# A graph message kernel: row fetches by byte address in four pieces, more of them, deferred loads, 14 slots and a shorter drain

## The chip, the core and the metric

The kernel runs on one core of one Trainium2 chip. The metric is device time in microseconds (us), the median of several executions. Engines are named as in the profile: PE (TensorE), DVE (VectorE), ACT (ScalarE), POOL (GpSimd), SP (SyncE). "SPq" and "ACTq" are the instructions with which SP and ACT start DMAs.

## What is computed

One message-passing layer on a graph of 6,250 nodes and 206,250 edges, sorted by receiver, feature width D = 128 in 8 heads of 16:

```python
w_ij = silu(edge_feats @ rad_W1 + rad_b1) @ rad_W2 + rad_b2
w_ij = w_ij + (silu(chi_scalar @ sph_W1 + sph_b1) @ sph_W2 + sph_b2)
q_i = (x @ Wq)[receivers];  k_j = (x @ Wk)[senders];  v_j = (x @ Wv)[senders]
alpha = (q_i * w_ij * k_j).sum(per head) / sqrt(16) * cutoffs
out = segment_sum(alpha * v_j, receivers) / 16
x = layernorm(x + out)
```

## The kernel before

**Prologue.** PE projects all nodes to keys and values; the table `kvtab` in HBM gets one row of 1 KB (key and value, 256 floats) per node. Then it projects the queries, which go to `qtab` as three bf16 parts. In this stretch SP and ACT also bring in index and weight arrays: the sender indices `srcS`, the edge weights `cutS` (which DVE multiplies by 1/64 at L425), the receiver indices, and the tables of row numbers `rowsS` and `rowsA`.

**Main loop.** The edges go in NE = 403 groups of 512 edges, each of four tiles of 128 edges. For a group:
- POOL gathers the sender rows of `kvtab`, one indirect DMA per tile (L540), into one of KS = 13 slots of `kvt`. A slot is free when DVE has made the messages of the group 13 before (wait on `m_msg`). The first HX = 6 groups need no such gather (`kvh`, made in the prologue). For the group in which POOL first uses a slot again, group HX + KS = 19, it waits for the messages of group 6.
- In some groups the fourth tile isn't gathered by POOL. Its 128 rows come one by one, each by a DMA of its own, RS = 7 rows a group from SP into `kvS` (L510) and RA = 8 a group from ACT into `kvA` (L629; 4 behind the two SiLUs of an even group, 12 behind those of an odd one). `row_tiles` says which groups these are: 21 fed by SP and 25 by ACT, so that POOL has 397 x 4 - 46 = 1542 gathers. The row number comes from a register, which a TENSOR_LOAD fills for four groups at once (28 registers on SP, 32 on ACT); a register instruction (named ISA below) makes the address from it.
- SP further issues, for each group, the query rows `qwt` (L516, behind a wait for the queries' matmul `m_q` of five groups earlier), and every four groups the edge features `eft` (L321, ES = 4 buffers) and the receivers `dbt` (L327).
- PE makes the hidden layer (L552, for two groups at once), the second layer `w_ij` (L575, L577), spreads the queries to edges (L565), sums messages by receiver (L585 into one bank, `SB`) and folds the four tiles (L591). ACT applies SiLU (L614). DVE multiplies weights and keys (`t1`, L708), then queries (L716), reduces per head (L718), makes the one-hot matrices (L640, L646), scales by the cutoff (L730), makes messages (L736), copies the sums to `part` (L655) and adds them to `accT` (L662).

PE sums group g - 3 while it works on group g, since `accumulate` of one group must end before the next may write `SB`. After the last group three groups are still to be summed, each by the same round of PE and DVE through the one bank. Then come three updates of window arrays, used only if the program loops again, the barrier, and the layernorm: PE centres (L799), ACT squares and takes roots (L810, L816), DVE scales (L834), SP stores.

What orders the work is the program text of each engine, joined by semaphores.

## Time and profile before

| | us |
|---|---|
| median of 3 runs | 2017.05 |
| lowest, highest | 2016.06, 2017.72 |
| the profiled execution | 2016.91 |
| its span, first to last instruction | 2015.6 |
| mean granted clock of PE | 0.932 of full speed |

| engine | busy us | share of the span |
|---|---|---|
| PE | 1709.1 | 85% |
| DVE | 1495.3 | 74% |
| POOL | 1488.6 | 74% |
| ACT | 560.7 | 28% |

Instructions that issue DMAs, read registers or wait aren't counted as busy, so the busy time of SP, ACT and POOL says little of how full their instruction streams are. The timeline shows the issue instructions of SP and ACT as merged rows: "x7" with 2.80 us is the time from the start of the first to the end of the seventh. For POOL the "idle before" of a gather that waited for nothing is put down to "issue".

### The profile page before, as it was taken

How to read it: one execution, taken by the hardware profiler on the slowest of the kernel's cores; microseconds unless marked ns; L12 is line 12 of the kernel's file. 1: busy time of each engine (PE TensorE's matmuls, PEld its weight loads, DVE VectorE, ACT ScalarE, POOL GpSimd, SP SyncE). 2: the span in 40 equal slices, each digit the busy share in tenths (PEclk: the TensorE clock that was granted, in tenths of full speed). 3: DMA queues.
4: the chain of work that ended last, by engine and by line, in shares of the span. 5: the costliest groups of instructions: out<-in, count | busy, mean ns of one | idle time of the engine just before them, and what ended most of it. 6: DMA issues, size and time to landing. Idle time of an engine off the chain costs nothing. (4 is left out here: it accounts for less than half of the span.)

```text
span 2015.6 us, 59668 instructions
## 1 busy us (share of the span) xinstructions
PE 1709.1 (85%) x14497; PEld 1251.5 (62%) x14497; DVE 1495.3 (74%) x3816; ACT 560.7 (28%) x955; POOL 1488.6 (74%) x1575
## 2 busy tenths in 40 slices
PE   8688989888988888888887888889888888888886
PEld 7566666666666666566665666656656665666665
DVE  4587887888887777777777777768777776777775
ACT  5332322222222222222222222222222222222233
POOL 6767777777777777777777777777777777777772
PEclk9899999999999989989899989988899999899898
DMA  9856666665666656655656656565565656566554
GB/s 330 268 149 164 171 170 170 168 166 160 170 170 171 166 158 168 169 158 163 169 152 169 164 157 169 152 168 162 160 168 152 169 162 159 159 162 169 150 139 127
DMA packets 194752, 339.98 MB, mean 169 GB/s; under 512 B 81140, under 2 KB 107108, under 8 KB 194404
## 3 DMA queue, kind: packets, MB, share of 16 engines
q0 software_dynamic: 74784, 203.79, 37.5%
q1 hardware_dynamic: 112488, 127.77, 21.9%
q10 hardware_dynamic: 7132, 4.59, 1.0%
q8 instruction: 119, 1.95, 0.4%
q14 instruction: 229, 1.88, 0.3%
HBM read 321.03 MB, written 14.95 MB: 167 GB/s over the span
## 5 line engine op out<-in xcount | busy, mean ns | idle before, releaser
L540 POOL DMA_INDIRECT kvt<-kvtab,srcS x1542 | 1462.8, 949 | 482.1 <-issue 458.4
L614 ACT ACTIVATE hs<-bank,B 128x512 f32<-128x512 f32 x806 | 509.9, 684 | 1399.2 <-PE bank L552 954.6
L708 DVE TENSOR_TENSOR t<-bank,kvt 128x512 f32<-128x512 f32 (+1 forms) x397 | 268.3, 676 | 398.3 <-DMA kvt<-kvtab,srcS 218.1
L575 PE MATMUL bank<-W2r,hs 128*128 128x128 f32 x3224 | 512.8, 307 | 8.9 <-ACT hs L614 8.9
L575 PEld LDWEIGHTS bank<-W2r,hs 128*128 128x128 f32 x3224 | 430.7, 208 | 97.2 <-issue 79.2
L575 PE MATMUL bank<-W2s,hs 128*128 128x128 f32 x3224 | 460.5, 290 | 0.0
L575 PEld LDWEIGHTS bank<-W2s,hs 128*128 128x128 f32 x3224 | 429.6, 207 | 0.0
L585 PE MATMUL bank<-msg,oh 128*32 128x128 f32 x3224 | 180.9, 296 | 245.3 <-DVE accT L662 240.7
L585 PEld LDWEIGHTS bank<-msg,oh 128*32 128x32 f32 x3224 | 71.9, 110 | 437.5 <-issue 437.5
L718 DVE TENSOR_REDUCE bank<-t 128x32 f32<-128x512 f32 x403 | 279.9, 695 | 13.9
L716 DVE TENSOR_TENSOR t<-bank,t 128x512 f32<-128x512 f32 x403 | 273.3, 678 | 17.5 <-PE bank L565 16.4
L736 DVE TENSOR_TENSOR msg<-kvt,bank 128x512 f32<-128x512 f32 (+1 forms) x397 | 266.6, 671 | 13.6
L552 PE MATMUL bank<-eft,W 32*128 32x512 f32 x1612 | 243.0, 671 | 0.9 <-DMA eft<-in_ef 0.9
L591 PEld LDWEIGHTS bank<-cS,part 128*128 128x128 f32 x806 | 122.5, 191 | 97.2 <-issue 94.0
L565 PE MATMUL bank<-qwt,ot 96*128 96x128 bf16 x1612 | 159.4, 221 | 23.8 <-issue 23.7
L591 PE MATMUL bank<-cS,part 128*128 128x32 f32 x806 | 167.6, 291 | 2.0 <-DVE part L655 2.0
L577 PE MATMUL bank<-b2p,ones 3*128 3x512 bf16 x403 | 158.5, 393 | 0.0
L640 DVE TENSOR_SCALAR ot<-dbt,basep 96x512 bf16<-96x512 int16 x403 | 150.2, 373 | 8.8 <-DMA qtab<-qx 8.1
L565 PEld LDWEIGHTS bank<-qwt,ot 96*128 96x128 bf16 x1612 | 131.1, 119 | 26.0 <-issue 26.0
L655 DVE COPY part<-bank 128x128 f32<-128x128 f32 x403 | 114.0, 283 | 13.1 <-PE bank L585 13.0
L646 DVE TENSOR_TENSOR oh<-cS,rel 128x128 f32<-128x128 f32 x403 | 114.0, 283 | 0.0
L552 PEld LDWEIGHTS bank<-eft,W 32*128 32x128 f32 x1612 | 65.8, 190 | 23.6 <-issue 2.2
(79 smaller groups left out, 491.4 us busy)
## 6 DMA issues: line engine op xcount, KB each, us to landing
eft<-in_ef SPq DMA_DIRECT2D x103, 512.0 KB
kvA<-kvtab ACTq DMA_DIRECT2D x3200, 1.0 KB
kvS<-kvtab SPq DMA_DIRECT2D x2688, 1.0 KB
dbt<-dst SPq DMA_DIRECT2D x102, 384.0 KB
kvt<-kvtab,srcS POOLq DMA_INDIRECT x1542
qwt<-qtab SPq DMA_DIRECT2D x403, 24.0 KB
kvtab<-kvt SPq DMA_DIRECT2D x24, 256.0 KB, 7.1
qtab<-qx SPq DMA_DIRECT2D x12, 384.0 KB, 8.6
```

The lines of the kernel that those rows point to most:

```text
L540: pool.indirect_dma_start(kvt[:, (g - HX) % KS, t, :], None, kvtab, bass.IndirectOffsetOnAxis(ap=srcS[:, g * TG + t:g * TG + t + 1], axis= ...
L552: pe.matmul(HB[i][:, :], W1[32 * i:32 * i + 32, :], eft[32 * i:32 * i + 32, q % ES, p % 2, :], start=True, stop=True).then_inc(m_l1, 1)
L565: m = pe.matmul(QB[:, t * D:(t + 1) * D], ot[:, g % OS, t * 128:(t + 1) * 128], qwt[:, g % QS, :], start=True, stop=True)
L575: pe.matmul(WB[g % 2][:, t * D:(t + 1) * D], hs[:, g % HS, j, t * 128:(t + 1) * 128], w2[:, :], start=(j == 0 and t == 0), stop=False, ski ...
L577: pe.matmul(WB[g % 2][:, :], ones3[:, :], b2p[:, :], start=False, stop=True, skip_group_check=True).then_inc(m_w, 1)
L585: m = pe.matmul(SB[32 * t:32 * t + W, 0:D], oh[:, g % MS, t, :], msg[:, g % MS, t, :], start=True, stop=True)
L591: pe.matmul(SB[:, D:D + W], part[:, g % 2, :], fold, start=True, stop=True).then_inc(m_fold, 1)
L614: act.activation(hs[:, g % HS, j, :], HB[i % 4][:, :], ACT.Silu, bias=B1[:, j:j + 1]).then_inc(m_si, 1)
L708: m = dve.tensor_tensor(t1[:, s, a:b, :], tiles(WB[s][:, :])[:, a:b, :], kv[:, :, 0:D], ALU.mult)
L716: dve.tensor_tensor(t2[:, s, :, :], tiles(QB[:, :]), t1[:, s, :, :], ALU.mult).then_inc(m_t2, 1)
L718: dve.tensor_reduce(alpha(g), t2[:, s, :, :].rearrange("p t (h d) -> p (t h) d", h=H), AX.X, ALU.add).then_inc(m_rd, 1)
L736: m = dve.tensor_tensor(msg[:, g % MS, a:b, :].rearrange("p t (h d) -> p t h d", h=H), kv[:, :, D:2 * D].rearrange("p t (h d) -> p t h d", ...
```

## The change

- RS and RA go from 7 and 8 to 9 and 10. 28 groups get their fourth tile from SP and 31 from ACT, POOL has 397 x 4 - 59 = 1529 gathers. Fetched tiles now lie in groups 15, 16, 28, 30, ...; the last two groups, 401 and 402, have four gathers each (402 had three).
- DVE multiplies the row numbers by 1024 in the prologue, so that a register holds the byte offset, and the DMA takes it directly. The register instruction in front of each row fetch goes, and of each `qwt` DMA too (`baseq`). A row is described as 4 x 256 bytes on both sides; `kvS` and `kvA` are laid out so. The registers are filled for two groups at once, 20 of them (18 used on SP, 20 on ACT).
- KS goes from 13 to 14, ES from 4 to 3.
- The bulk of `srcS` and `cutS` is loaded by ACT after its part of the query projection, where SP loaded both in the middle of it; the first 64 columns of `cutS` still come from SP. The factor 1/64 moves into the constant `fold`, and DVE's multiplication and its wait for `cutS` go.
- The last two groups are summed in banks of their own (`strips`), so that their sums don't wait for `accumulate`; the window updates are placed between steps that wait; `oh` of the last group and the update of `rel` come ahead of its wait for the gather.
- The two instructions of DVE for a fetched tile take it as two halves of 64 floats.
- After the barrier ACT takes one root of a constant (`rooted`) ahead of the layernorm's squares, so that the function table is loaded there.

```diff
-RS, RA = 7, 8
+RS, RA = 9, 10
+LS, LA = -(-2 * RS // 4) * 4, -(-2 * RA // 4) * 4
...
-    KS, ES, DS, QS, HS, MS, OS = 13, 4, 3, 6, 4, 4, 3
+    KS, ES, DS, QS, HS, MS, OS = 14, 3, 3, 6, 4, 4, 3
...
+    KVROW, QROW = 4 * 2 * D, 2 * NPART * D
+    kv_bytes = kvtab.rearrange("n f -> (n f)").bitcast(u8)
+    q_bytes = qtab.rearrange("n f -> (n f)").bitcast(u8)
...
-        rowsS = sb("rowsS", [NG // 4, 4 * RS], i32)
-        rowsA = sb("rowsA", [NG // 4, 4 * RA], i32)
-        kvS = sb("kvS", [128, 2, 2 * D], f32)
-        kvA = sb("kvA", [128, 2, 2 * D], f32)
+        rowsS = sb("rowsS", [NG // 4, 2 * LS], i32)
+        rowsA = sb("rowsA", [NG // 4, 2 * LA], i32)
+        kvS = sb("kvS", [128, 4, 2, D // 2], f32)
+        kvA = sb("kvA", [128, 4, 2, D // 2], f32)
         kvt = sb("kvt", [128, KS, TG, 2 * D], f32)
-        dbt = sb("dbt", [WP, DS, 4, G], i16)
+        dbt = sb("dbt", [128, DS, 4, G], i16)
...
-                if b == min(9, NQB):
-                    dve.wait_ge(s_cut, 16)
-                    dve.tensor_scalar(cutS[:, :], cutS[:, :], 1.0 / 64.0, None, ALU.mult).then_inc(s_win, 1)
...
-                if b == min(4, NQB - 1):
-                    sp.dma_start(srcS[:, SE:T], srcT[:, SE:T]).then_inc(s_src2, 16)
                 if b == min(5, NQB - 1):
-                    sp.dma_start(cutS[:, :], cutT).then_inc(s_cut, 16)
+                    sp.dma_start(cutS[:, 0:SE], cutT[:, 0:SE]).then_inc(s_cut, 16)
...
-                    features(1)
+            if NQP > 1:
+                features(1)
             dve.wait_ge(s_win, 4)
 
+            act.dma_start(srcS[:, SE:T], srcT[:, SE:T]).then_inc(s_src2, 16)
+            act.dma_start(cutS[:, SE:T], cutT[:, SE:T]).then_inc(s_cut2, 16)
+            dve.wait_ge(s_rows, 32)
+            for rows in (rowsS, rowsA):
+                dve.tensor_scalar(rows[:, :], rows[:, :], float(KVROW), None, ALU.mult).then_inc(s_bytes, 1)
+            dve.wait_ge(s_cut, 16)
...
+            def kv_row(reg):
+                return kv_bytes[bass.ds(start_of(reg, (N - 1) * KVROW), KVROW)].rearrange("(o a f) -> o a f", o=1, a=4)
 
             def sp_rows(g):
-                if g % 4 == 0:
-                    sp.load(sp_row, rowsS[g // 4:g // 4 + 1, :])
+                if g % 2 == 0:
+                    sp.load(sp_row, rowsS[g // 4:g // 4 + 1, g % 4 // 2 * LS:(g % 4 // 2 + 1) * LS])
                 for r in range(RS * g, RS * (g + 1)):
                     u, p = r // 128, r % 128
                     if u < len(at_s):
                         if p == 0 and u >= 2:
                             sp.wait_ge(m_msg, at_s[u - 2] + 1)
-                        row = sp.snap(sp_row[r % (4 * RS)], min_val=0, max_val=N - 1)
-                        sp.dma_start(kvS[p:p + 1, u % 2, :], kvtab[bass.ds(row, 1), :]).then_inc(m_kvS[u % 2], 16)
+                        sp.dma_start(kvS[p:p + 1, :, u % 2, :].bitcast(u8), kv_row(sp_row[r % (2 * RS)])
+                                     ).then_inc(m_kvS[u % 2], 16)
 
             def query_rows(g):
                 if g >= QS:
                     sp.wait_ge(m_q, g - QS + 1)
-                at = window_start(sp, sp_base, g)
-                sp.dma_start(qwt[:, g % QS, :],
-                             qtab[bass.ds(at, W), :].rearrange("n (c f) -> (n c) f", c=NPART)
+                if g % 4 == 0:
+                    sp.load(sp_base, baseq[0:1, g:g + 4])
+                at = start_of(sp_base[g % 4], (NQ - W) * QROW)
+                sp.dma_start(qwt[:, g % QS, :].bitcast(u8),
+                             q_bytes[bass.ds(at, W * QROW)].rearrange("(n f) -> n f", n=W * NPART)
...
+            def strips(g):
+                return HB[NE - 1 - g] if g >= NE - 2 else SB
+
             def scat(g):
                 pe.wait_ge(m_msg, g + 1)
-                if g >= 1:
+                if g >= NE - 2:
+                    pe.wait_ge(m_si, 2 * NE)
+                elif g >= 1:
                     pe.wait_ge(m_acc, g)
                 for t in range(TG):
-                    m = pe.matmul(SB[32 * t:32 * t + W, 0:D], oh[:, g % MS, t, :], msg[:, g % MS, t, :],
+                    m = pe.matmul(strips(g)[32 * t:32 * t + W, 0:D], oh[:, g % MS, t, :], msg[:, g % MS, t, :],
                                   start=True, stop=True)
                 m.then_inc(m_sc, 1)
 
             def fold_tiles(g):
                 pe.wait_ge(m_part, g + 1)
-                pe.matmul(SB[:, D:D + W], part[:, g % 2, :], fold, start=True, stop=True).then_inc(m_fold, 1)
+                pe.matmul(strips(g)[:, D:D + W], part[:, g % 2, :], fold, start=True, stop=True).then_inc(m_fold, 1)
...
+            scat(NE - 3)
+            scat(NE - 2)
+            fold_tiles(NE - 3)
+            fold_tiles(NE - 2)
+            scat(NE - 1)
+            fold_tiles(NE - 1)
...
+            def next_rel():
+                dve.wait_ge(m_oh, NE)
+                dve.tensor_scalar(rel[:, :], rel[:, :], -float(W), None, ALU.add).then_inc(m_up, 1)
...
+            def next_base():
                 dve.wait_ge(m_q, NE)
-                dve.wait_ge(m_oh, NE)
                 dve.tensor_scalar(base[:, :], base[:, :], float(W), None, ALU.add).then_inc(m_up, 1)
+                dve.wait_ge(m_up, 2)
+                dve.tensor_copy(basei[:, :], base[0:1, :]).then_inc(m_up, 1)
+                dve.tensor_scalar(baseq[:, :], base[0:1, :], float(QROW), None, ALU.mult).then_inc(m_up, 1)
+
+            def next_basep():
                 dve.tensor_scalar(basep[:, :], basep[:, :], float(W), None, ALU.add).then_inc(m_up, 1)
-                dve.tensor_scalar(rel[:, :], rel[:, :], -float(W), None, ALU.add).then_inc(m_up, 1)
...
+                if g == NE - 1:
                     window(g)
-                if g == NE:
-                    next_windows()
-                if g >= NE:
+                    next_rel()
...
+                n, kv, row = gathered(g), kv_rows(g), alone(g)
+                m = dve.tensor_tensor(t1[:, s, 0:n, :], tiles(WB[s][:, :])[:, 0:n, :], kv[:, 0:n, 0:D], ALU.mult)
+                if row is not None:
+                    m = dve.tensor_tensor(halves(t1[:, s, KT, :]), halves(WB[s][:, KT * D:TG * D]), row[:, 0:2, :],
+                                          ALU.mult)
...
+            collect(NE - 2)
+            accumulate(NE - 3)
+            accumulate(NE - 2)
+            next_base()
+            collect(NE - 1)
+            next_basep()
+            accumulate(NE - 1)
...
+            act.activation(rooted[:, :], eps[:, :], ACT.Sqrt)
...
-    cst[:, 4 + W + 256:] = np.tile(np.eye(W), (128 // W, 1))
+    cst[:, 4 + W + 256:] = np.tile(np.eye(W), (128 // W, 1)) / 64.0
```

The two streams of SP in the steady loop, one row per instruction: `kvS` is a row fetch, ISA the register instruction, `qwt` the query rows. Before:

```order
L510 DMA kvS<-kvtab 1x256
L499 ISA
L516 DMA qwt<-qtab 96x128
L509 ISA
L510 DMA kvS<-kvtab 1x256
```

SP in the changed kernel, for four groups (L328 is `eft`, L334 `dbt`):

```order
L528 DMA qwt<-qtab 96x256
L328 DMA eft<-in_ef 128x2x512
L334 DMA dbt<-dst 96x2048
L513 TENSOR_LOAD rowsS
L519 DMA kvS<-kvtab 1x4x256 x9
L528 DMA qwt<-qtab 96x256
L519 DMA kvS<-kvtab 1x4x256 x9
L528 DMA qwt<-qtab 96x256
L513 TENSOR_LOAD rowsS
L519 DMA kvS<-kvtab 1x4x256 x9
```

The register instructions are gone, nine fetches follow each other directly, and there are two loads of registers for four groups where there was one.

PE at the end of the loop, where L585 sums a group's messages and L591 folds them; before:

```order
L565 MATMUL bank<-qwt,ot 128x128 x4
L585 MATMUL bank<-msg,oh 32x128 x4
L591 MATMUL bank<-cS,part 128x32
L585 MATMUL bank<-msg,oh 32x128 x4
L591 MATMUL bank<-cS,part 128x32
L585 MATMUL bank<-msg,oh 32x128 x4
L591 MATMUL bank<-cS,part 128x32
```

And in the changed kernel (L602 and L608):

```order
L577 MATMUL bank<-qwt,ot 128x128 x4
L602 MATMUL bank<-msg,oh 32x128 x8
L608 MATMUL bank<-cS,part 128x32 x2
L602 MATMUL bank<-msg,oh 32x128 x4
L608 MATMUL bank<-cS,part 128x32
```

Groups 400 and 401 are now summed one behind the other, and only group 402 makes a round of its own.

## Rows read from the trace of the kernel before

**Rows 1.** The page's costliest groups: POOL's gathers.

```profile
L540 POOL DMA_INDIRECT kvt<-kvtab,srcS x1542 | 1462.8, 949 | 482.1 <-issue 458.4
```

**Rows 2.** Waits of the whole span: total us, times, longest us.

```profile
POOL kvt L540 <- issue: 458.4, 1503, 0.3
DVE t L708 <- DMA kvt<-kvtab,srcS: 218.1, 129, 4.4
DVE t L708 <- PE bank L577: 180.2, 222, 4.8
POOL kvt L540 <- DVE msg L736: 19.1, 38, 6.3
```

**Rows 3.** Timeline of POOL: start us, us, operation, idle before and releaser.

```profile
39.47 0.94 POOL L540 DMA_INDIRECT kvt<-kvtab,srcS  x1 [4.62 <-DMA kvtab<-kvt]
...
110.46 0.94 POOL L540 DMA_INDIRECT kvt<-kvtab,srcS  x1 [6.30 <-DVE msg L736]
...
116.84 0.95 POOL L540 DMA_INDIRECT kvt<-kvtab,srcS  x1 [1.68 <-DVE msg L736]
...
1978.81 0.95 POOL L540 DMA_INDIRECT kvt<-kvtab,srcS  x1 [0.30 <-issue]
```

**Rows 4.** Timeline of SP's issues in the loop, four groups' special ones among them.

```profile
87.61 2.74 SPq L510 DMA_DIRECT2D kvS<-kvtab  x7
91.16 0.32 SPq L516 DMA_DIRECT2D qwt<-qtab  x1
...
1504.13 0.44 SPq L321 DMA_DIRECT2D eft<-in_ef  x1
1504.62 0.49 SPq L327 DMA_DIRECT2D dbt<-dst  x1
1507.22 2.80 SPq L510 DMA_DIRECT2D kvS<-kvtab  x7
```

**Rows 5.** Timeline of ACT's issues: a load onto three partitions, row fetches.

```profile
3.25 0.25 ACTq L214 DMA_DIRECT2D b2w<-in_b2s  x1
...
1510.96 0.63 ACTq L629 DMA_DIRECT2D kvA<-kvtab  x2
...
1511.76 3.81 ACTq L629 DMA_DIRECT2D kvA<-kvtab  x10
```

**Rows 6.** Timeline of the prologue's end.

```profile
61.73 1.00 DVE L425 TENSOR_SCALAR cutS<-cutS 128x1616 f32<-128x1616 f32 x1 [5.89 <-DMA cutS<-in_cutT]
...
76.47 0.61 DVE L640 TENSOR_SCALAR ot<-dbt,basep 96x512 bf16<-96x512 int16 x2 [8.15 <-DMA qtab<-qx]
```

**Rows 7.** Timeline of the last group and the drain.

```profile
1981.64 0.56 DVE L708 TENSOR_TENSOR t<-bank,kvt 128x384 f32<-128x384 f32 x1 [0.40 <-DMA kvt<-kvtab,srcS]
...
1984.85 0.28 DVE L736 TENSOR_TENSOR msg<-kvA,bank 128x128 f32<-128x128 f32 x1
...
1987.55 0.29 DVE L655 COPY part<-bank 128x128 f32<-128x128 f32 x1 [0.86 <-PE bank L585]
...
1988.67 0.19 DVE L662 TENSOR_TENSOR accT<-accT,bank 128x32 f32 x1 [0.83 <-PE bank L591]
...
1990.94 0.35 DVE L743 CAST basei<-base 1x404 int32<-1x404 f32 x1
...
1992.64 12.89 PE L799 MATMUL bank<-cS,accT 128*128 128x128 f32 x98 [1.94 <-PEq L751]
```

**Rows 8.** The chain that ended last, in order of time: the layernorm's start.

```profile
1992.64 3.75 PE bank L799 x16
...
1997.58 1.28 ACT L816
...
1998.87 0.31 ACT sd L816
```

**Rows 9.** Stretch of the main loop: us, busy per engine, clock, DMA share, GB/s.

```profile
81.00:1979.00 1898.00, 1631.34 (x14031) 1183.37 (x14030) 1439.66 (x3697) 508.09 (x804) 1430.30 (x1510) 0.94 0.60 162
```

More of the change, by code:

```diff
@@ L104, in gnn_program @@
         basei = sb("basei", [1, NG], i32)
+        baseq = sb("baseq", [1, NG], i32)
         npass = sb("npass", [1, 1], i32)
@@ L679, in kv_rows, with alone, halves @@
                 return kvt[:, (g - HX) % KS, :, :]
[L681 to L682 removed]
+            def alone(g):
                 if g in use_s:
[L684 removed]
+                    return kvS[:, :, use_s[g] % 2, :]
                 if g in use_a:
[L686 to L687 removed]
+                    return kvA[:, :, use_a[g] % 2, :]
+                return None
+            def halves(t):
+                return t.rearrange("p (c f) -> p c f", c=2)
             def alpha(g):
```

161 lines of the change are left out of this document (79 added, 82 removed).

## The prediction, made before the changed kernel ran

> **What bounds the kernel now.** The share of busy time points at PE (85%) and says little, so I read the waits first. DVE's first step of a group waits 218.1 us for gathered rows, in 129 of 397 groups, and 180.2 us for PE [rows 2]. A wait for rows can come from late transfers or from late issue, so the second view is POOL. It has 1542 gathers of 949 ns, and 458.4 us of idle time between them in pieces of at most 0.3 us, which is its own issue time [rows 1, 2]. The timeline gives the sum directly: from the first gather at 39.47 to the last at 1978.81 are 1939.3 us for 1541 steps [rows 3]. POOL really waited in only two places worth naming, 6.30 and 1.68 us, of which 0.30 each is the ordinary gap: 7.4 us, both before 117 us, when its slots had filled ahead of the first groups. So a step costs (1939.3 - 7.4) / 1541 = 1.2537 us, and after 117 us POOL never pauses for anyone. When PE falls behind, as in the stretches of low clock, DVE lags some groups and catches up; that costs nothing as long as POOL isn't stopped by full slots, and it isn't.
>
> The time is therefore: start of the gathers (39.5), 1542 steps, the first stalls, and what follows the last gather. The last gather starts at 1978.81, its group begins on DVE at 1981.64, the last update is done at 1991.3, PE's centring starts at 1992.64 [rows 3, 7], and the layernorm ends the span at 2015.6.
>
> **The change, part by part**, against the profiled execution's own 2016.91 us (1.3 above its span, 0.14 below the median of 2017.05, so nothing has to be shifted).
>
> 1. *Fewer gathers.* 1542 - 1529 = 13 steps of 1.2537 us: **-16.3**. They lie on the path that sets the end, all of them. The instruction itself is the same.
>
> 2. *The first stalls.* POOL was ready for slot 1's second use at 110.46 - 6.00 = 104.5 and got it at 110.46. With a fourteenth slot, and two fetched tiles (groups 15, 16) before that point where one was (18), it makes 54 gathers first and not 51, and asks at 108.2. It then wants the messages of group 7 at 113.2, which came at 116.5. So without any faster start 3.3 us of stall remain of 7.4. The start should be faster too: DVE's wait of 5.89 us for `cutS` and the 1.0 us multiplication go [rows 6]. The next step needed the queries' projection, which other waits held as well, so I count that the query chain is some 3 us or more ahead and the two big loads no longer delay the last writes of `qtab`, for which DVE waited 8.15 us until 76.47 [rows 6]. 3.3 us earlier is enough to end the stall. Against it: ACT now issues the loads just behind, beside those same writes. Bounds: all 7.4 gained, or, if the start comes 4 us later, nothing. I take **-7.4**, since the cleared wait is in a row and the delay isn't.
>
> 3. *The drain.* From the last gather to its group's first step nothing changes (2.83 us, landing). `oh` and the update of `rel` are put ahead of it; group 401 had its rows four gathers, 5.0 us, earlier, and needs 3.4 us (1981.64 to 1985.13, rows 7), so the 1.1 us fit in the gap and cover is there. With full four tiles and without `oh`, group 402 is some 0.3 shorter. After its messages (1985.13): before, 6.2 us to the end of the last cast. Now: copy to fold to update for group 401, as in 1987.55 to 1988.67, 1.1 us plus 0.2; then base, basei and baseq at 0.35 each, 1.1; meanwhile PE has summed group 402; then copy, fold, update again, 1.3. That makes 3.8 and not 6.2 [rows 7]. **-2.7** together; bounds 0 (if the two new waits cost as much as they save) and -3.5.
>
> 4. *The root.* The table load of 1.28 us stands in the chain between squares and first root [rows 8]; ahead of the squares it lies under PE's first centring, 3.75 us for two blocks in the chain. After it DVE is the busy one to the end, so everything moves up: **-1.3**. The Trainium skill ("ScalarE: Activation LUTs", What ACT_TABLE_LOAD costs) gives 2.66 us for a switch, the load and a drain of 1.38. The row shows the load alone, with 0.01 us behind it. By the page the sum would be 1.4 us lower.
>
> 5. *What SP and ACT pay for the rates.* This decides whether part 1 stands. Two fetches take 0.63 us and ten 3.81 [rows 5]: one each (3.81 - 0.63) / 8 = 0.40, the issue itself 0.23, the rest gap and register instruction. Without that instruction only a gap as between two plain issues stays, 0.05 (eft to dbt, rows 4). How long the issue of four pieces is no row shows. Below: 0.23 (one piece). Above: 0.32, the 96 pieces of `qwt` [rows 4]. Nearest: 0.25, a load onto three partitions [rows 5]. So a fetch costs p = 0.28 to 0.37, and I take 0.30, less than the 0.40 now. Registers: the load of 28 took 1507.22 - 1505.11 = 2.11, less an ordinary 0.19, 1.92; the one of 4 took 0.62 (91.16 - 90.35, less 0.19); 20 are then about 1.5. For four groups SP has 36 fetches, four `qwt` with their gaps (0.42 each), `eft` and `dbt` (1.03), two loads of 20 and one of 4: 36p + 1.7 + 1.03 + 3.0 + 0.6 = 36p + 6.3, so 17.1 us at 0.30. From its start at about 77 to the end of the gathers at 1955 a group may take (1955 - 77) / 403 = 4.66, four of them 18.6. It fits, with 1.5 us left; before it was about 17.6 of 18.9. ACT has 20p + 1.5 = 7.5 for two groups beside its SiLUs, before 16 x 0.40 + 1.1 = 7.5. Cost **0**, covered by POOL; the cover is gone at p = 0.34.
>
> 6. *The rest at nothing.* ES = 3 makes SP wait at every fourth group until PE's first layer of the group before is done: it is then three to four groups ahead and not five, and behind that wait stand `dbt`, a register load and nine fetches, wanted four groups later. DVE's two halves have the same element count, and DVE waits for rows anyway. POOL needs the rest of `srcS` at its group 16, at about 88; ACT issues that load before 70. More pieces for the queues: their engines are busy 0.60 of the loop [rows 9].
>
> Sum: 16.3 + 7.4 + 2.7 + 1.3 = 27.7, and 2016.9 - 27.7 = **1989.2 us**, 1.4% faster.
>
> **Rivals.**
>
> - *A. SP becomes the bound (slower).* Place: the row fetches and `qwt` behind them, for which PE's L565 would wait in every group. Price: each 0.01 us of p above 0.34 adds 0.09 us a group, 36 us in all. Slower than before from p = 0.35. At the upper bound 0.37 a group takes 4.9 us and the time is about 1989 + 403 x 0.25 = 2090. For it: the margin is 8% and the issue of this form is in no row. Against it: the three-piece load at 0.25, and that a piece count of 96 only gives 0.32. Chance 0.10.
>
> - *B. The first stall stays*, since the deferred 1.6 MB come down on the last `qtab` writes: 1989.2 + 7.4 = 1996.6, or 1992.5 if only the slot helps. For it: DVE waited 8.15 us for their landing while bulk loads ran. Chance 0.20.
>
> - *C. The gathers stretch.* Every row now is four pieces, 30,208 where there were 5,888; they use the same transfer engines as POOL's gathers. If a step grows by 0.01 us, 1529 of them cost 15: about 2004. Against it: at a DMA share of 0.60 [rows 9] the mean step, 1.2537, is 949 ns and the 0.30 of issue to within 0.005 [rows 1, 3]: nothing stretched it so far. The Trainium skill ("DMA: Bandwidth & Descriptors", Specifications) says that below 512 bytes a transfer is read, modified and written, which speaks against such pieces; no row here times one piece alone. Chance 0.06.
>
> - *D. The change doesn't do what it says*, or PE's pace hides the 13 gathers: between 2013 and 2017. But the count of gathers is fixed by the plan, and PE is busy 1631 us and DVE 1440 us in the loop's 403 groups, 4.05 and 3.57 us a group [rows 9], under the 4.66. Chance 0.02.
>
> **How the numbers follow.** The forecast (1984 to 1994) has 0.62. Its lower end adds the larger bounds of parts 3 and 4, about 1985, and 1984 for a step nearer 1.250. With B the mass reaches 1998; half of C lies within 1999. Range 1984 to 1999 leaves out A, D and the rest of C, and a little at the low end. A measurement of this kernel tells 0.2% from no change: faster by more than that has 0.62 + 0.20 + 0.06 = 0.88, the same 0.02, slower 0.10.
>
> **What would show it.** Right: POOL's gathers x1529 at 949 ns, first start near 39.5, last near 1955; its waits for DVE near nothing; DVE still waits for rows, not for `qwt` or `kvS`; fetches of 0.30 us, nine in under 2.8; 11 us and not 13.8 from the last gather to PE's centring; no table load behind the squares. Wrong: PE waiting for DMA at the queries' matmul, DVE's L742 released by `kvS` or `kvA`, or POOL's step above 1.26.

## The result, and the profile after

| | us |
|---|---|
| kernel before, median of 4 runs of the comparison | 2017.38 (2016.06 to 2020.03) |
| changed kernel, median of 4 runs | 3542.88 (3540.14 to 3548.99) |
| ratio, with its 95% interval | 1.756 (1.7535 to 1.759) |
| profiled execution, its span | 3544.71, 3543.0 |

The change makes the kernel slower by 1525 us. The forecast was 1989.2 and the range ended at 1999. The likeliest case was wrong. The rival "SP becomes the bound" had the right kind of cause, the issue of the row fetches, but a price far too low and, for the changed kernel itself, the wrong place: PE waits for ACT there and not at the queries' matmul.

The costliest groups of the changed kernel (same columns as [rows 1]; the releaser at the end is what ended most of the idle time). L552 is what L540 was, L635 the SiLUs, L587 the second layer, L742 DVE's first step of a group:

```profile
L552 POOL DMA_INDIRECT kvt<-kvtab,srcS x1529 | 1447.1, 946 | 1945.2 <-DVE msg L770 1318.0
...
L635 ACT ACTIVATE hs<-bank,B 128x512 f32<-128x512 f32 x806 | 509.3, 683 | 2937.2 <-issue 2076.2
L742 DVE TENSOR_TENSOR t<-bank,kvt 128x512 f32<-128x512 f32 (+1 forms) x397 | 266.6, 671 | 1594.3 <-PE bank L589 1267.6
```

And its waits (total us, times, longest), to be read against [rows 2]:

```profile
ACT hs L635 <- issue: 2076.2, 225, 10.5
POOL kvt L552 <- DVE msg L770: 1318.0, 299, 29.0
DVE t L742 <- PE bank L589: 1275.1, 298, 8.4
...
PE bank L587 <- ACT hs L635: 763.1, 194, 11.8
...
ACT hs L635 <- PE bank L589: 801.1, 169, 5.3
```

Read backwards this is one queue. POOL's 1529 gathers still take 946 ns each, but now POOL stands 1318 us waiting for DVE to free slots. DVE waits 1275 us for PE's second layer, PE waits 763 us for the hidden layer from ACT, and ACT waits 2076 us for "issue", that is for nothing but its own instruction stream. The 801 us that are put down to PE's L589 are of the same kind: the idle time of an engine counts its own DMA issues in. In the timeline below the SiLU at 1506.59 has 4.66 us of it, and ACT's fifth fetch before it ended at 1506.48. Taken instruction by instruction, with issues and register loads counted as occupied, ACT's stream waits for another engine nowhere between 110 and 3498 us (no gap over 0.35 us). The timeline of ACT and SP shows what fills that stream (start us, us, operation; idle before and releaser):

```profile
1500.67 1.26 ACT L635 ACTIVATE hs<-bank,B 128x512 f32<-128x512 f32 x2 [10.02 <-issue]
...
1501.98 2.08 PE L587 MATMUL bank<-W2r,hs 128*128 128x128 f32 x8 [4.49 <-ACT hs L635]
...
1502.71 3.77 ACTq L649 DMA_DIRECT2D kvA<-kvtab  x5
1503.21 6.83 SPq L519 DMA_DIRECT2D kvS<-kvtab  x9
...
1506.59 0.69 ACT L635 ACTIVATE hs<-bank,B 128x512 f32<-128x512 f32 x1 [4.66 <-PE bank L589]
1506.69 0.58 ACTq L649 DMA_DIRECT2D kvA<-kvtab  x1
...
1507.37 10.25 ACTq L649 DMA_DIRECT2D kvA<-kvtab  x14
...
1511.68 6.37 SPq L519 DMA_DIRECT2D kvS<-kvtab  x9
1517.72 1.26 ACT L635 ACTIVATE hs<-bank,B 128x512 f32<-128x512 f32 x2 [9.87 <-issue]
```

One fetch costs 0.58 us by itself and 0.71 to 0.76 in a row of them, where ten took 3.81 before, register instructions included [rows 5], and where the prediction took 0.30. From 1500.67 to 1517.72, two groups of ACT, are 17.05 us, of which 3.77 + 0.58 + 10.25 = 14.6 us are twenty fetches; a register load of 1.9 us takes most of the rest. At this pace the loop's 201.5 pairs of groups take 3436 of the 3543 us. SP is full as well: its `eft` of every fourth group stands at these times, 29 cycles apart:

```profile
315.14 0.43 SPq L328 DMA_DIRECT2D eft<-in_ef  x1
...
1312.65 0.42 SPq L328 DMA_DIRECT2D eft<-in_ef  x1
```

(1312.65 - 315.14) / 29 = 34.40 us for four groups, 8.60 each. Before, SP's cycle had room. Its waits in the kernel before, for the queries' matmul:

```profile
SPq L498 <- PE bank L565: 79.5, 35, 5.5
SPq L499 <- PE bank L565: 79.0, 47, 7.3
```

In the changed kernel nothing of the kind is left: the longest wait of SP in the loop is 0.5 us. So both streams are full, and over the loop they run at one pace, 17.2 us for two groups on ACT and 34.4 for four on SP. PE waits for ACT alone; its queries' matmul L577, for which SP fetches, has 0.2 us of wait. Why two streams of different content run at the same pace isn't shown.

The stretch of the loop, to be read against [rows 9] (us, busy of PE, weight loads, DVE, ACT, POOL, granted clock, DMA share, GB/s):

```profile
81.00:3500.00 3419.00, 2542.64 (x13932) 1833.90 (x13932) 1454.85 (x3697) 504.81 (x800) 1415.38 (x1497) 0.66 0.32 90
```

DVE and POOL do the same work as before (1455 and 1415 us). The transfer engines are busy 0.32 of the time and not 0.60, so the loss isn't in moving bytes. PE's busy time grew from 1631 to 2543 us because the granted clock fell from 0.94 to 0.66 of full speed, in a loop in which PE stood waiting for ACT: the eight matmuls of L587 in the timeline above take 2.08 us, at the lower of its two levels (1.2 GHz) and behind a wait of 4.49, where they take 1.16 in the one-piece kernels below at the higher (2.4 GHz). The lower clock doesn't set the time: ACT's stream never waits for PE there, and PE still has 763 us of wait for ACT left over.

### The profile page after: what moved, and what is told of

The parts are those of the page before. It is cut to its first block and busy times, and to the rows that moved or that the text cites. A ratio compares the mean times of both kernels' runs of the same rounds, so it can differ in the third digit from the quotient of the medians.

```text
span 3543.0 us, 56930 instructions
## 1 busy us (share of the span) xinstructions
PE 2629.3 (74%) x14497; PEld 1908.5 (54%) x14497; DVE 1520.9 (43%) x3845; ACT 560.3 (16%) x956; POOL 1472.3 (42%) x1562
## 5 line engine op out<-in xcount | busy, mean ns | idle before, releaser
L552 POOL DMA_INDIRECT kvt<-kvtab,srcS x1529 | 1447.1, 946 | 1945.2 <-DVE msg L770 1318.0
L587 PE MATMUL bank<-W2r,hs 128*128 128x128 f32 x3224 | 788.9, 421 | 786.7 <-ACT hs L635 763.1
L587 PEld LDWEIGHTS bank<-W2r,hs 128*128 128x128 f32 x3224 | 675.4, 310 | 913.5 <-ACT hs L635 823.4
L635 ACT ACTIVATE hs<-bank,B 128x512 f32<-128x512 f32 x806 | 509.3, 683 | 2937.2 <-issue 2076.2
L742 DVE TENSOR_TENSOR t<-bank,kvt 128x512 f32<-128x512 f32 (+1 forms) x397 | 266.6, 671 | 1594.3 <-PE bank L589 1267.6
L587 PE MATMUL bank<-W2s,hs 128*128 128x128 f32 x3224 | 693.6, 388 | 4.7 <-issue 4.7
L587 PEld LDWEIGHTS bank<-W2s,hs 128*128 128x128 f32 x3224 | 670.7, 306 | 4.5 <-issue 4.4
L564 PE MATMUL bank<-eft,W 32*128 32x512 f32 x1612 | 548.7, 890 | 5.1 <-ACT hs L635 2.4
L602 PE MATMUL bank<-msg,oh 128*32 128x128 f32 x3224 | 210.5, 340 | 95.6 <-DVE accT L685 48.2
L564 PEld LDWEIGHTS bank<-eft,W 32*128 32x128 f32 x1612 | 207.4, 243 | 122.6 <-ACT hs L635 79.5
L602 PEld LDWEIGHTS bank<-msg,oh 128*32 128x32 f32 x3224 | 76.6, 121 | 365.3 <-issue 364.5
L608 PEld LDWEIGHTS bank<-cS,part 128*128 128x128 f32 x806 | 146.5, 228 | 130.6 <-issue 126.6
L608 PE MATMUL bank<-cS,part 128*128 128x32 f32 x806 | 194.2, 327 | 2.4 <-DVE part L676 2.4
L589 PE MATMUL bank<-b2p,ones 3*128 3x512 bf16 x403 | 193.0, 479 | 0.3 <-issue 0.3
L577 PE MATMUL bank<-qwt,ot 96*128 96x128 bf16 x1612 | 183.7, 246 | 0.2 <-DVE t L753 0.2
L577 PEld LDWEIGHTS bank<-qwt,ot 96*128 96x128 bf16 x1612 | 158.4, 137 | 1.1 <-DVE t L753 0.7
```

Source lines behind the costliest of these rows:

```text
L552: pool.indirect_dma_start(kvt[:, (g - HX) % KS, t, :], None, kvtab, bass.IndirectOffsetOnAxis(ap=srcS[:, g * TG + t:g * TG + t + 1], axis= ...
L564: pe.matmul(HB[i][:, :], W1[32 * i:32 * i + 32, :], eft[32 * i:32 * i + 32, q % ES, p % 2, :], start=True, stop=True).then_inc(m_l1, 1)
L577: m = pe.matmul(QB[:, t * D:(t + 1) * D], ot[:, g % OS, t * 128:(t + 1) * 128], qwt[:, g % QS, :], start=True, stop=True)
L587: pe.matmul(WB[g % 2][:, t * D:(t + 1) * D], hs[:, g % HS, j, t * 128:(t + 1) * 128], w2[:, :], start=(j == 0 and t == 0), stop=False, ski ...
L589: pe.matmul(WB[g % 2][:, :], ones3[:, :], b2p[:, :], start=False, stop=True, skip_group_check=True).then_inc(m_w, 1)
L602: m = pe.matmul(strips(g)[32 * t:32 * t + W, 0:D], oh[:, g % MS, t, :], msg[:, g % MS, t, :], start=True, stop=True)
```

## The experiments

**The two kernels again.** A repeat of both, each against the kernel before.

> The kernel before itself, unchanged, for its trace on this chip. On two chips every kernel with rows in one piece stood near 3080 us, this one too, and in their traces the transfers issued by SP and ACT stood still for 5 to 12 us at a time, some 90 times in all, while POOL's gathers went on. If that belongs to the chip and not to an edit, this trace shows the same standstills where the time is near 3080, and none where it is near 2017.

Measured: 2015.55 us, beside 2017.79 for the kernel before in that comparison.

> The changed kernel itself, unchanged. Theory: it is bound by SP's and ACT's own issue of the four-piece fetches, 0.66 to 0.78 us each, so its time hardly depends on the chip: 3540 us within 3%, where the kernel before has 2017 and where it has 3080. Rival: it pays the standstills of a slow chip on top, 3540 + 1000.

Measured: 3544.07 us. ACT again waits 2112.0 us for its own issues and POOL 1318.9 us for DVE. The result is a property of the kernel.

**One piece and not four.** This undoes the piece count alone; byte addresses, 9 and 10 rows, slots, loads and drain stay:

```diff
-        kvS = sb("kvS", [128, 4, 2, D // 2], f32)
-        kvA = sb("kvA", [128, 4, 2, D // 2], f32)
+        kvS = sb("kvS", [128, 2, 2 * D], f32)
+        kvA = sb("kvA", [128, 2, 2 * D], f32)
...
-                return kv_bytes[bass.ds(start_of(reg, (N - 1) * KVROW), KVROW)].rearrange("(o a f) -> o a f", o=1, a=4)
+                return kv_bytes[bass.ds(start_of(reg, (N - 1) * KVROW), KVROW)].rearrange("(o f) -> o f", o=1)
```

> The change with each row fetch as one piece of 1024 bytes on both sides, all else as in the change (byte addresses, 9 and 10 rows a group, 14 slots, loads, drain). On another chip such a fetch took 0.31 to 0.33 us in a row of them, inside my bounds. Theory (the pieces alone turned the sign): SP's four groups are 36 x 0.32 + 6.3 = 17.8 us, under the 18.6 that POOL's pace allows, and the parts of the prediction other than the piece count hold: 1989 us, between 1984 and 1999; after the last gather 36 us or so instead of 37.7. Rival (9 and 10 rows a group are too many for SP and ACT whatever their form): over 2030 us, ACT hs and DVE waiting for issue. Rival (the saving of gathers is eaten by other waits): within 0.2% of the kernel before.

Measured: 2061.34 us (2060.0 to 2062.51), the kernel before 2016.94; ratio 1.0222 (1.0204 to 1.0239). Of 1525 us of loss the pieces alone carry 1481. But it isn't the 1989 of my theory either: it is the first rival of this run. What waits is another engine than that rival said: the queries' matmul, behind SP's stream (rows below). So the prediction had two faults, and the second would have turned its sign alone.

**The same at 7 and 8 rows.**

```diff
-RS, RA = 9, 10
+RS, RA = 7, 8
```

> As e11_one_piece, but with 7 and 8 rows a group as in the kernel before, so that POOL has 1542 gathers again. By the prediction's terms this leaves the first stalls (7.4), the drain (2.7) and the root (1.3): 2016.9 - 11.4 = 2005.5 us, and 16.3 us more than e11_one_piece. If it is as fast as e11_one_piece, the thirteen gathers bring nothing; if it is level with the kernel before, the other edits bring nothing.

Measured: 2007.05 us (2006.22 to 2008.66), ratio 0.9951 (0.9935 to 0.9968). The expected 2005.5 is 1.6 away: the edits other than fetches, taken together, bring about what was forecast. Its trace lets me read each of them (below).

**Four pieces in the kernel before**, all else as before; DVE takes the fetched tile in halves.

```diff
-        kvS = sb("kvS", [128, 2, 2 * D], f32)
-        kvA = sb("kvA", [128, 2, 2 * D], f32)
+        kvS = sb("kvS", [128, 4, 2, D // 2], f32)
+        kvA = sb("kvA", [128, 4, 2, D // 2], f32)
...
-                        sp.dma_start(kvS[p:p + 1, u % 2, :], kvtab[bass.ds(row, 1), :])
+                        sp.dma_start(kvS[p:p + 1, :, u % 2, :], kvtab[bass.ds(row, 1), :].rearrange("o (a f) -> o a f", a=4))
```

> The kernel before with one edit: each row fetch described as 4 x 256 bytes, kvS and kvA laid out for it, DVE taking the fetched tile in halves. Rates, addresses, slots, loads and drain as before. Theory (a description of more than one dimension costs SP and ACT a fixed time at each issue): a fetch and its register instruction took 0.76 us in a row of them on another chip; SP's four groups are 28 x (0.66 to 0.80) + 6.3 = 24.8 to 28.7 us, 6.2 to 7.2 a group, so 2580 to 2980 us. Rival (the pieces cost only together with the higher rates or the byte addresses): within 2% of the kernel before.

Measured: 3002.14 us in one run, 22 us above the upper end of what was expected (2580 to 2980). The pieces need neither the byte addresses nor the higher rates to do their harm, and with elements of 4 bytes a lone fetch costs the same 0.58 us. Timeline of SP and ACT:

```profile
1503.07 5.33 SPq L510 DMA_DIRECT2D kvS<-kvtab  x7
1503.11 8.06 ACTq L629 DMA_DIRECT2D kvA<-kvtab  x11
...
1520.35 0.58 ACTq L629 DMA_DIRECT2D kvA<-kvtab  x1
```

Seven fetches take 5.33 us where the same line took 2.80 [rows 4]. With seven and eight rows SP's stream is the longer one, and here PE waits where the rival had said, at the queries' matmul L565:

```profile
PE bank L565 <- issue: 770.7, 239, 7.2
```

That it is SP's issue stream that it waits for shows in the timeline: at nine in ten of these waits it starts 1.7 to 2.8 us behind the issue of its `qwt` rows, which take 1.9 us to land. In the changed kernel it starts 13 us behind (medians).

**Two pieces of 512 bytes** in the changed kernel.

```diff
-        kvS = sb("kvS", [128, 4, 2, D // 2], f32)
+        kvS = sb("kvS", [128, 2, 2, D], f32)
...
-                return kv_bytes[bass.ds(start_of(reg, (N - 1) * KVROW), KVROW)].rearrange("(o a f) -> o a f", o=1, a=4)
+                return kv_bytes[bass.ds(start_of(reg, (N - 1) * KVROW), KVROW)].rearrange("(o a f) -> o a f", o=1, a=2)
```

> The change with two pieces of 512 bytes instead of four of 256. Theory (the cost is that of the second dimension, whatever its count): as slow as the change, 3543 us within some 2%. Rival (each piece has its price, as by the count of packets): half of the loss, about 2760 us. Second rival (pieces under 512 bytes are what is slow): near e11_one_piece.

Measured: 3518.49 us in one run. Half the pieces, the same time: the price isn't one for each piece. Timeline rows of SP and ACT:

```profile
1508.76 6.62 SPq L519 DMA_DIRECT2D kvS<-kvtab  x9
1511.46 0.57 ACTq L649 DMA_DIRECT2D kvA<-kvtab  x1
1512.12 10.10 ACTq L649 DMA_DIRECT2D kvA<-kvtab  x14
```

0.57 us alone and 10.10 for fourteen, against 0.58 and 10.25 with four pieces. The page's queue of ACT says that the pieces themselves were made as written (packets, MB, share): before, changed, two pieces.

```profile
q10 hardware_dynamic: 7132, 4.59, 1.0%
```

```profile
q10 hardware_dynamic: 32764, 7.02, 1.0%
```

```profile
q10 hardware_dynamic: 16892, 6.99, 0.7%
```

With one piece and the changed kernel's rates (the one-piece kernel above) that row has 8956 packets. 3968 fetches with two pieces add 7936, two each, and with four pieces 23808, six each: every piece brings a packet of data and one of completion. The Trainium skill ("DMA: Bandwidth & Descriptors", Why a DMA increments its semaphore by 16 and not by 1) says that such a copy runs on the largest number of engines up to 16 that divides the outermost count on both sides, and that each of them posts its own completion; the packet counts agree. The number of packets doubles between these two kernels and the issue costs the same, so it isn't their number that SP and ACT pay for. No run has pieces on one side of the copy alone, so which side costs is open.

**Which engine binds at 9 and 10 rows.** Four kernels as the one-piece kernel with other rates, one line each: `RS, RA = 9, 8`, `7, 10`, `8, 9` and `8, 10`. In their comparison the kernel before took 2020.62 us (2015.31 to 2023.29), so the ratios say more than the times.

> The change with rows in one piece, 9 rows a group on SP and 8 on ACT, 1535 gathers. Theory (SP's stream of issues is the bound at 9 rows: four groups take 36 x 0.335 + 6.5 = 18.6 us plus about 0.9 of stretched issues, measured 4.87 us a group from the first group on): still about 2040 to 2061 us. Rival (ACT's ten rows are what is too many): 2007.05 - 7 x 1.2537 = 1998.3 us.

Measured: 2004.71 us in two runs, ratio 0.9919 (0.9899 to 0.9939). My theory falls: nine rows on SP beside eight on ACT do no harm.

> As e15, with 7 rows a group on SP and 10 on ACT, 1536 gathers. Theory: SP's four groups are 28 x 0.335 + 6.5 = 15.9 us, POOL stays the bound: 2007.05 - 6 x 1.2537 = 1999.5 us. Rival (ACT is the bound at 10): about 2045 to 2061 us.

Measured: 2004.65 us (1997.86 to 2007.65), ratio 0.9924 (0.9907 to 0.994). Ten rows on ACT beside seven on SP do none either.

> As e15, with 8 and 9 rows a group, 1535 gathers. Theory: SP's four groups are 32 x 0.335 + 6.5 = 17.2 us, 18.1 with the stretch of e11, of 18.7 that POOL's pace allows: 2007.05 - 7 x 1.2537 = 1998.3 us, with next to no margin. Rival (the stretched issues grow with the two rates and pass the allowance): over 2010 us.

Measured: 2003.39 us (1998.83 to 2005.07), ratio 0.9915 (0.9899 to 0.9932).

> As e15, with 8 and 10 rows a group, 1532 gathers. Theory (SP alone decides): 2007.05 - 10 x 1.2537 = 1994.5 us. Rival (ACT's ten rows beside SP's eight stretch SP's issues): over 2005 us.

Measured: 2003.28 us (2000.76 to 2005.4), ratio 0.9908 (0.9891 to 0.9924), between the theory's 1994.5 and the rival's 2005.

So it takes both. The traces say how. `eft` times of SP, first the kernel with 9 and 10 rows, 51 cycles apart:

```profile
300.72 0.42 SPq L328 DMA_DIRECT2D eft<-in_ef  x1
...
1294.75 0.42 SPq L328 DMA_DIRECT2D eft<-in_ef  x1
```

then 9 and 8 rows, 54 cycles apart:

```profile
294.84 0.42 SPq L328 DMA_DIRECT2D eft<-in_ef  x1
...
1287.77 0.42 SPq L328 DMA_DIRECT2D eft<-in_ef  x1
```

Four groups cost SP 994.03 / 51 = 19.49 us with ten rows on ACT and 992.93 / 54 = 18.39 with eight. The prediction allowed 18.6. SP's instructions are the same in both, but its nine fetches take longer. With ten rows on ACT the 398 runs of nine fetches have a median of 2.91 us and a mean of 3.16 (longest ones over 6); with eight they have 2.85 and 2.91. Four of them at 0.25 more make the 1.0 us. One long run of nine, timeline of the kernel with 9 and 10 rows:

```profile
1512.67 2.85 SPq L519 DMA_DIRECT2D kvS<-kvtab  x9
...
1517.50 6.39 SPq L519 DMA_DIRECT2D kvS<-kvtab  x9
```

In the long run of nine single issues of SP lasted 1.42 and 1.34 us where the ordinary one is 0.23; there is no wait in it. ACT's issues beside it stayed at 0.235 us until 1520.3. What the runs of fetches of SP lie above their median in all goes with ACT's rate: 15 us at 7 and 8 rows and 21 at 9 and 8, 31 at 8 and 9, 60 at 7 and 10, 84 at 8 and 10, 102 at 9 and 10. At 7 or 8 rows SP has room for them. Overlap with ACT's fetches alone doesn't bring them: at 7 and 8 rows 374 of SP's 384 runs of fetches overlap ACT's and none is stretched by over 0.6 us.

The trace has one thing more that goes with them. A `qwt` load is spread over the transfer engines and tells its end by sixteen completions, one by one. From its issue to the fifteenth and to the sixteenth (medians of the loads behind 200 us of which all sixteen are in the trace; the last column is the time above the median from the paragraph before):

| kernel, rows of SP and ACT | fifteenth us | sixteenth us | stretched us |
|---|---|---|---|
| kernel before, 7 and 8 | 1.97 | 4.50 | 12 |
| one piece, 7 and 8 | 1.94 | 4.90 | 15 |
| one piece, 9 and 8 | 1.89 | 5.01 | 21 |
| one piece, 8 and 9 | 1.92 | 7.27 | 31 |
| one piece, 7 and 10 | 2.01 | 7.28 | 60 |
| one piece, 8 and 10 | 1.91 | 13.97 | 84 |
| one piece, 9 and 10 | 1.97 | 15.25 | 102 |
| four pieces, 9 and 10 | 2.00 | 2.08 | |

So one of the sixteen parts of a load comes late, and only with fetches in one piece. The likely reading is that these fetches all run on one transfer engine, which has too much to do while the other fifteen have room. The data packets of ACT's fetches with 9 and 10 rows fit it: they come one at a time (1 of 3923 overlaps another), where with four pieces 4203 of 15753 overlap. The trace doesn't name the engine of a packet, so that reading is argued. SP's stretched issues stand where the late part is latest: with 9 and 10 rows 66 of the 85 issues of over 0.6 us come when `qwt` lands over 12 us late, with 8 and 10 rows 64 of 70. That the full engine holds up the issue fits this, but no run shows it by itself.

What waits for SP is the queries' matmul L577, by its `qwt` rows. At each of the 90 waits of over 0.5 us with 9 and 10 rows it starts 0.09 us behind their landing, though SP had issued them 15 to 19 us before. SP itself waits for nothing, and its stream with the stretched issues has the pace of the kernel (4 x 4.87 us); whether SP or a full engine sets that pace can't be told apart here. The waits of the kernel with 9 and 10 rows:

```profile
PE bank L577 <- issue: 203.6, 94, 5.6
...
DVE t L753 <- PE bank L577: 161.6, 88, 4.8
```

and of the one with 9 and 8:

```profile
PE bank L577 <- issue: 59.6, 37, 3.1
DVE t L753 <- PE bank L577: 44.9, 27, 3.0
```

**The same kernels on two other chips.** Eight runs, made ahead of the others, fell on two chips on which the kernel before itself takes 3080 to 3096 us, so that the sign of a small change there can't be carried over. Their expectations were made before this was known, and no time below is to be held against them. The names say which of the kernels above it is: one piece, four pieces only, two pieces, one piece at 7 and 8 rows.

> The changed kernel, but each fetched row is described as one piece of 1024 bytes (kvS and kvA laid out as before); byte addresses from the register, rates 9 and 10, deferred loads, 14 slots and the short drain stay. Theory 1 (issuing four pieces is what costs; after, a fetch takes about 0.76 us of SP's and ACT's stream): a fetch costs 0.28 to 0.30, POOL bounds again, 1989 us. Rival 2 (taking the byte address straight from the register, or fetches with no register instruction between them, is what costs): it stays near 3540 us. Rival 3 (one-byte elements cost, whatever the pieces): also near 3540.

Measured: 3098.68 us, the kernel before 3096.14 there; ratio 1.0015 (0.9997 to 1.0034).

> The kernel before, rates 7 and 8, register instruction kept, 4-byte elements, and only the pieces changed: each row lands as four pieces of 256 bytes in kvS and kvA. Theory 1: a fetch then costs 0.76 us or, with the register instruction on top, up to 0.9. SP has 28 fetches and 6.3 us of other work for four groups, so 27.6 to 31.5 us, 6.9 to 7.9 a group, 403 groups and 120 us around them: 2900 to 3300 us. Rivals 2 and 3 (direct address, one-byte elements): 2017 us, as before.

Measured: 3632.82 us in one run.

> The changed kernel with two pieces of 512 bytes a row in place of four of 256. If the issue's cost goes by the number of pieces (0.23 for one, about 0.7 for four with both queues at work), two take 0.39 and with the gap 0.45: SP 36 x 0.45 + 6.3 = 22.5 us for four groups, 5.6 a group, 2380 us. If it is a fixed price for a second dimension, whatever its size, about 3540. If pieces below 512 bytes were the cost (read, modify, write), 1989.

Measured: 3919.66 us in one run.

> The changed kernel with one piece a row and the old rates 7 and 8, so the deferred loads, the 14 slots, the drain, the root and the byte addresses alone. By the parts of the prediction: 2016.9 - 7.4 (first stalls) - 2.7 (drain) - 1.3 (root) = 2005.5 us. If the deferred loads hold up the start, 2013.

Measured: 3084.70 us, ratio 0.9955 (0.9937 to 0.9973).

On the second chip the kernel before took 3079.95 us.

> The changed kernel with one piece of 1024 bytes a row, once more, beside a run of the kernel before at 2017 (in the first comparison every kernel, the one before too, ran above 3000 us on its chip). A single fetch with one piece took 0.23 us there and with two or four pieces 0.57 and 0.58. Theory 1, now: a second dimension in the description costs 0.34 us an issue, whatever its size, and this alone makes the change slow. Then this kernel takes 1989 us, as the prediction's other parts say. Rival 2 (direct addresses or the higher rates cost as well): between 2017 and 3540.

Measured: 3072.46 us, ratio 0.9975 (0.9955 to 0.9995).

> The kernel before, only with four pieces a row. Theory 1: a fetch costs 0.66 (0.58 and a gap) to 0.80 us. SP 28 fetches and 6.3 us for four groups, 6.2 to 7.2 us a group: 2620 to 3020 us. Rival 2: 2017.

Measured: 3622.32 us in one run.

> The changed kernel with one piece a row and rates 7 and 8: deferred loads, 14 slots, drain, root and byte addresses without the 13 gathers. By the prediction's parts 2005.5 us; 16.3 above the kernel with one piece and rates 9 and 10.

Measured: 3055.11 us, ratio 0.9923 (0.9899 to 0.9947).

The eighth run takes the changed kernel and gives ACT's rows one piece, so that SP alone has four:

```diff
-                        act.dma_start(kvA[p:p + 1, :, u % 2, :].bitcast(u8), kv_row(act_row[r % (2 * RA)])
+                        act.dma_start(kvA[p:p + 1, u % 2, :].bitcast(u8), kv_whole(act_row[r % (2 * RA)])
```

> The changed kernel with four pieces on SP's rows alone; ACT's rows come in one piece. In the changed kernel a lone fetch took 0.58 us, but nine on SP 6.8, 0.78 each, while ACT issued too. If the rest is the two queues hindering each other in the longer form, SP's nine now take 0.66 each, 5.9 us, 36 x 0.66 + 6.3 = 30 for four groups, 7.5 a group, 3140 us. If it is SP's own, 0.78 and 3540.

Measured: 3419.17 us in one run. That lies between the expected 3140 and 3540. Nine of SP's fetches took a median of 6.06 us there, 0.67 each, where the changed kernel has 6.50 with both queues in pieces. So SP's own pieces make the most of its price, and ACT's add some. SP's pieces alone also bind the kernel, at 8.12 us a group beside 8.60 in the changed one: PE again waits at the queries' matmul, L580 in this kernel.

```profile
PE bank L580 <- issue: 945.9, 233, 8.1
```

The counterpart, four pieces on ACT alone, has no run.

What those two chips did shows in the one-piece kernel at 7 and 8 rows on the first of them. Its waits, and a stretch of its timeline:

```profile
DVE t L742 <- remote: 879.8, 126, 8.7
PE bank L602 <- DVE accT L685: 807.5, 164, 9.2
ACT hs L635 <- remote: 760.0, 77, 14.3
```

```profile
1498.87 0.95 POOL L552 DMA_INDIRECT kvt<-kvtab,srcS  x1 [0.30 <-issue]
...
1503.87 0.94 POOL L552 DMA_INDIRECT kvt<-kvtab,srcS  x1 [0.30 <-issue]
1506.64 0.00 SPq L528 DMA_DIRECT2D qwt<-qtab  x1
1506.84 0.69 DVE L742 TENSOR_TENSOR t<-bank,kvt 128x512 f32<-128x512 f32 x1 [8.48 <-remote]
1506.97 1.26 ACT L635 ACTIVATE hs<-bank,B 128x512 f32<-128x512 f32 x2 [10.65 <-remote]
```

Transfers that SP and ACT had issued all but stood still for 5 to 12 us at a time while POOL's gathers went on at their 1.25 us. SP's queue has 33 to 82 gaps of over 5 us between its packets in each of the four one-piece runs on these chips, and none to four in the one-piece runs on the others. With two or four pieces the queue has at most four such gaps, on any chip. The gaps don't add up to the 1050 us by which these chips are slower (the longer ones make at most 690 us in a run). Why stays open.

## Where the prediction was right and where it failed

**Part 5 failed, in its bound.** The structure held: four groups of SP cost 36p + 6.3 us and the cover ends at 18.6. With 9 and 8 rows SP's cycle of 18.39 is 36 x 0.332 + 6.4 (nine fetches in 2.91 us and their gap, by nine). What failed is "So a fetch costs p = 0.28 to 0.37". Its upper end came from `qwt` with 96 pieces and its likely value from a load onto three partitions [rows 4, 5]; both lie one piece to a partition. No row of the trace of before has several pieces within a single partition. It has rows with several in each of 128 partitions, and the prediction passed them over (issues of `eft` with two pieces a partition and of `out` with four; least, median and longest ns):

```profile
L321 SPq DMA_DIRECT2D eft<-in_ef x103: 379/427/1551, 58.0 to 1993.2; - x103
...
L849 SPq DMA_DIRECT2D out<-kvt x12: 372/372/1038, 2000.1 to 2011.6; - x12
```

And the other load onto three partitions, just ahead of the one that gave 0.25, took more than twice as long:

```profile
L214 ACTq DMA_DIRECT2D b2w<-in_b2r x1: 568/568/568, 2.7 to 2.7; - x1
```

At 0.43 and the gap of 0.05 the rival's formula already gives 2487 us. Even these rows don't show 0.58, so the bound had to stay open above, and the rival needed more than 0.10. The measured 34.40 us is p = 0.78 by the prediction's sum (the fetches and their gaps take 0.74 each, and the other work 7.8 us and not 6.3). Put into the rival's own formula, 1989 + 403 x (34.40 / 4 - 4.66) = 3577 us, 1% from the result. So the price was mis-sized by more than a factor of two.

The rival's place came true only where SP's stream is the longer one (pieces at 7 and 8 rows, or on SP alone). In the changed kernel the step "ACT has 20p + 1.5 = 7.5 for two groups" failed with it: fetches and register load take 16.5 us there, and it is ACT for which PE waits.

**The cover was thinner than it looked.** "It fits, with 1.5 us left" used 17.1 us. Its gap of 0.05 us between two fetches came from `eft` and `dbt` [rows 4]. Both kernels have one more register instruction, a MOVE, in front of each fetch, and the change takes out only the other. The kernel with one piece and 9 and 10 rows (least, median and longest ns):

```profile
L519 SPq MOVE kvS<-kvtab x3584: 29/29/29, 77.0 to 2004.0; - x200
```

So the gap is 0.10, and a fetch of one piece costs 0.33 and not 0.28 to 0.30: at the 0.34 where the cover ends. With one piece SP needs 18.4, and 19.5 when ACT issues ten rows a group. By the same formula 19.49 gives 1989 + 403 x 0.21 = 2075; measured 2061. A stream filled to 92% by a sum of unloaded issue times had no room for issues that stretch under load, which no row of the loop before showed either: SP's seven fetches there have a median of 2.78 us and lie 12 us above it in all. Nor did part 5 or part 6 ask whether one of the sixteen transfer engines could be full while they are busy 0.60 on average; the late sixteenth completion says that one nearly was, before the change too. The "about 17.6 us" that SP needed before the change come to 16.5 from the terms named (28 x 0.40 + 1.7 + 1.03 + 1.92 + 0.6); nothing else rests on them.

**Part 1, the gathers, holds.** The step stays at 1.250 to 1.258 us in every kernel where POOL doesn't wait. From 7 and 8 rows to 8 and 9, seven gathers fewer, the last gather moves from 1972.88 to 1964.58, 8.3 us for an expected 8.8. In the kernel with 9 and 10 rows it stands at 1977.33, because POOL then waits for slots, and from there to the end are 81 us and not 33: the gathers had stopped being the bound.

**Parts 2 to 4 can be read in the one-piece kernel with 7 and 8 rows.** Timeline rows of its POOL, DVE, PE and ACT:

```profile
39.78 0.94 POOL L552 DMA_INDIRECT kvt<-kvtab,srcS  x1 [4.83 <-issue]
...
78.36 0.69 DVE L742 TENSOR_TENSOR t<-bank,kvh 128x512 f32<-128x512 f32 x1 [4.38 <-PE bank L589]
...
1972.88 0.95 POOL L552 DMA_INDIRECT kvt<-kvtab,srcS  x1 [0.30 <-issue]
...
1984.26 1.28 ACT L863 ACT_TABLE_LOAD   x1 [15.69 <-PEq L794]
1984.43 2.92 PE L842 MATMUL bank<-cS,accT 128*128 128x128 f32 x12 [1.32 <-PEq L794]
```

| part | predicted us | measured us | how |
|---|---|---|---|
| 2, first stalls | -7.4 | -5.9 | last gather 1978.81 to 1972.88; no wait for slots is left |
| 3, drain | -2.7 | -2.3 | last gather to PE's centring, 13.83 [rows 3, 7] to 11.55 |
| 4, root | -1.3 | -1.1 | centring to the end of the span, 22.96 to 21.87 |

Part 2 came 1.5 short: the first gather starts 0.3 us later, and two of the first four gathers last 0.5 to 0.6 us longer. The time of the last gather and the two stretches behind it make up the whole span, so their -9.3 is the whole difference, 2015.6 to 2006.3. For part 4 the 2.66 us of the Trainium skill ("ScalarE: Activation LUTs", What ACT_TABLE_LOAD costs) would have been too much; the load alone, as [rows 8] show it, is what went. Rival B, that the first stall stays, didn't come: the loop's first L742 runs at 78.36 us, where it ran at 81.89 before.

**Part 6 at nothing is right, as far as it can be read.** In this kernel SP does wait at L328, 318.0 us in 86 places, since `eft` has three buffers, and nothing waits for it: PE's L577 has no wait row of note. Transfers cost nothing extra either (rival C): gathers of 946 ns beside the four pieces. The rule of the Trainium skill ("DMA: Bandwidth & Descriptors", Specifications) on transfers below 512 bytes can't be the cause: two pieces of 512 cost as much as four of 256.

**What remains of the change.** Everything but the four pieces and the highest rates is worth having. One piece with 8 and 10 rows is at 0.9908 of the kernel before (0.9891 to 0.9924), with 8 and 9 at 0.9915 (0.9899 to 0.9932), and both beat the two kernels that were compared. They can't be told apart, nor from 9 and 8 or 7 and 10. The sums had 1994.5 and 1998.3 us for them, ratios 0.989 and 0.991.

## What to carry to other kernels

Before many small transfers are put on a queue, time one issue in the very form that is meant: an issue that is priced from another shape, even from one with more pieces, isn't priced. In this kernel a stream of issues planned to 92% full by unloaded times was full, so leave more room than that, and sum both issuing engines, with all that waits behind each. A mean share of 0.60 over sixteen transfer engines can hide one that is full, so look at how long a transfer takes to land, and at its last completion. And where a stall in the trace comes out as "issue", look at the issuing instructions of that engine: busy shares and transfer shares both fall while the kernel gets slower.

## What the runs showed of the hardware

- The issue of a row fetch of 1 KB onto one partition costs SP or ACT 0.23 us in one piece, 0.57 in two and 0.58 in four (one issue standing alone). Going from one piece to two costs 0.34 us, going from two to four next to nothing. The price belongs to this form: 96 pieces over 96 partitions cost 0.32 [rows 4], four pieces in each of 128 partitions 0.37 and two in each 0.43 (medians). One behind the other, the one-piece form takes 0.31 to 0.36 a fetch, the others 0.67 to 0.76.
- The issues of the two engines disturb each other: SP's nine one-piece fetches take 2.91 us on average beside eight rows a group on ACT, 3.16 beside ten, with single issues of 1.3 to 2.0 us. Of the issues of over 0.6 us in the four kernels with nine or ten rows on ACT 170 of 197 stand where a `qwt` load lands over 12 us behind its issue.
- With one-piece fetches the last of the sixteen completions of a `qwt` load comes 4.5 to 15 us behind the issue (medians), the later the more rows the fetches bring in a group, and the other fifteen within 2 us. With four pieces the sixteenth comes 2.1 us behind the issue.
- The Trainium skill ("DMA: Bandwidth & Descriptors", Issuing engines are not separate DMA queues) calls the time of initiating a DMA "usually small relative to the DMA itself". Here the issues of 1 KB rows set the time of the whole kernel, at a transfer share of 0.32. The packets of ACT's queue take 1.0% of 16 engines' 3543 us, by estimate 0.14 us of one engine for each of its 3968 fetches, where the issue takes 0.58 or more.
- On two chips transfers issued by SP and ACT all but stood still for 5 us and more at a time (up to 12.6) while the gathers went on, and all one-piece kernels took about 3050 to 3100 us.
